# Expert attention in a four-layer decoder: the order of the matmuls in each step, regrouped

## The reference

```python
q = rope(einsum('bsd,hdp->bhsp', x, Wq))
k = rope(einsum('bsd,hdp->bhsp', x, Wk))
gv = gate(x, Wsel_v)                      # sigmoid scores, all but the best 2 of 8 set to 0
v = einsum('bsd,bhse,hedp->bhsp', x, gv, Wv)
att = softmax(einsum('bhsp,bhtp->bhst', q, k) / sqrt(P), axis=-1)
o = einsum('bhst,bhtp->bhsp', att, v)
go = gate(x, Wsel_o)
out = einsum('bhsp,bhse,hepd->bsd', o, go, Wo)
```

## Time and profile before

| | us |
|---|---|
| Median of 3 runs | 2660.39 (2655.98 to 2660.68) |
| The profiled execution | 2660.01 |
| Its span | 2658.2 |
| TensorE busy | 2227.7 (84%) |
| VectorE busy | 1791.3 (67%) |
| ScalarE busy | 1241.8 (47%) |
| GpSimd busy | 1196.4 (45%) |
| Mean granted clock of TensorE | 0.902 of full speed |

### The profile page before, as it was taken

How to read it: one execution, slowest core, us unless ns; L and a number is a source line. 1 busy time by engine, 2 the same in 40 slices (tenths; PEclk the granted TensorE clock), 3 DMA queues, 4 the chain that set the end, 5 groups by cost and what they waited for, 6 DMA issues and landing times. The chain is left out here.

```text
span 2658.2 us, 43969 instructions
## 1 busy us (share of the span) xinstructions
PE 2227.7 (84%) x13502; PEld 1582.2 (60%) x13502; DVE 1791.3 (67%) x3827; ACT 1241.8 (47%) x2557; POOL 1196.4 (45%) x1377
## 2 busy tenths in 40 slices
PE   6888759663999975749999999989999867699698
PEld 3666547453788853636656556655666445499555
DVE  4667658556688856666776676767677555477598
ACT  6777535222566642225445344534444432244365
POOL 5331028001699920127666565756575100022298
PEclk8999869775999998769999999999999977699799
DMA  1000024000666600013344343334333400000184
GB/s 45 2 2 2 7 57 100 7 6 19 140 153 153 150 4 18 1 63 80 80 84 92 77 98 75 96 65 96 77 84 79 87 6 0 32 1 1 25 176 101
DMA packets 63008, 162.17 MB, mean 61 GB/s; under 512 B 7563, under 2 KB 18571, under 8 KB 55000
## 3 DMA queue, kind: packets, MB, share of 16 engines
q1 hardware_dynamic: 62792, 159.50, 26.8%
HBM read 156.46 MB, written 3.01 MB: 60 GB/s over the span
## 5 line engine op out<-in xcount | busy, mean ns | idle before, releaser
L1984 PE MATMUL bank<-l2h_og,l2h_wo 128*128 128x512 f32 x512 | 264.2, 600 | 12.0 <-DVE LNT L2228 11.3
L2086 ACT ACTIVATE l2h_pr<-twin,l2h_nmx 128x512 f32<-128x512 f32 x256 | 176.0, 688 | 173.6 <-PE bank L1973 122.3
L2078 ACT ACTIVATE l2h_prT<-bank 128x512 f32<-128x512 f32 x256 | 151.7, 592 | 213.1 <-PE bank L1973 213.1
L1075 POOL TENSOR_TENSOR l1m_hid_lo<-l1m_hid,l1m_hid_hi 128x512 fp32r<-128x512 f32 x136 | 217.2, 1617 | 62.1 <-ACT l1m_hid_hi L1054 61.4
L2231 DVE TENSOR_REDUCE l2h_nmx<-twin 128x2 f32<-128x1024 f32 x128 | 156.2, 1220 | 104.5 <-PE twin L1963 103.8
L2204 DVE TENSOR_TENSOR l2h_vg<-bank,l2h_gv 128x512 f32<-128x512 f32 x256 | 175.4, 685 | 54.6 <-POOL l2h_vs L2299 32.0
L2299 POOL TENSOR_TENSOR l2h_vs<-l2h_vg 128x256 f32<-128x256 f32 x256 | 190.8, 745 | 27.9 <-DVE l2h_vg L2204 27.7
L2294 POOL TENSOR_TENSOR l2h_plain<-l2h_plain,l2h_rotated 128x512 f32<-128x512 f32 x64 | 82.0, 1281 | 213.9 <-DVE l2h_rotated L2197 213.9
L2216 DVE TENSOR_TENSOR l2h_og<-bank,l2h_gt 128x512 f32<-128x512 f32 x256 | 173.2, 680 | 5.3 <-PE bank L1984 2.7
L1973 PE MATMUL bank<-ident,l2h_pr 128*128 128x128 f32 x1024 | 163.4, 282 | 2.5 <-issue 2.5
L1973 PEld LDWEIGHTS bank<-ident,l2h_pr 128*128 128x128 f32 x1024 | 119.0, 143 | 71.4 <-issue 54.8
(11 more groups left out here) (636 smaller groups left out, 6199.1 us busy)
## 6 DMA issues: line engine op xcount, KB each, us to landing
l2h_gt<-l2m_gate_rows SPq DMA_DIRECT2D x128, 512.0 KB, 7.1
l1m_c<-l1m_weights SPq DMA_DIRECT2D x64, 512.0 KB, 6.3
l3m_c<-l3m_weights SPq DMA_DIRECT2D x32, 512.0 KB, 6.6
l0m_c<-l0m_weights SPq DMA_DIRECT2D x16, 512.0 KB, 6.8
l1m_w<-in_l1m_pairs SPq DMA_DIRECT2D x32, 192.0 KB, 6.2
l2h_fresh<-in_l2m_wqkv SPq DMA_DIRECT2D x8, 768.0 KB, 4.9
l2h_wo<-in_l2m_wo SPq DMA_DIRECT2D x8, 512.0 KB, 4.8
l0m_w<-in_l0m_pairs SPq DMA_DIRECT2D x8, 192.0 KB, 5.0
```

What stands on the lines that cost most here:

```text
L1075: nc.gpsimd.tensor_tensor(hid_lo[:, at, :], hid[:, (n + PRE) % 4, :], hid_hi[:, at, :], ALU.subtract)\
L1984: nc.tensor.matmul(ybank[:, :], wo[s][:, e, :], og[:, e % 4, :], start=(e == 0), stop=(e == E - 1))\
L2078: nc.scalar.activation(prT[:, j // 2 % 2, h, :, j % 2 * P:(j % 2 + 1) * P], tbank[:, :].rearrange("p (c q) -> p c q", c=TPB), ACT.Copy).th ...
L2086: nc.scalar.activation(pr[:, h, :], sbank[:, h, :], ACT.Exp, bias=nmx[:, k % 2, h:h + 1], accum_out=rs[:, g % 2, t, h:h + 1]).then_inc(exp ...
```

## The change

The matmuls of a step are regrouped. The order before was score, turn 0, piece 0, project 0, piece 1, turn 1, piece 2, project 1; it becomes score, piece 0, turn 0, project 0, turn 1, piece 1, piece 2, project 1. What follows (weighing, factor, gates) stays. VectorE's order follows: the second gate product now comes after the third take. No instruction is added or removed, and the waits are those of before, in new places.

```diff
@@ TensorE, step
                         if due(k, 0, last):
                             score(it, k)
+                        for g, n in pieces[0:1]:
+                            make(it, g, n, last)
                         if due(k, 1, last):
                             if 1 <= q <= B and not last:
                                 pe.wait_ge(go_copied, it * B + B + q)
                             turn_probs(it, k - 1, 0)
-                        for g, n in pieces[0:1]:
-                            make(it, g, n, last)
                         if due(k, YLAG, last):
                             project(it, (k - YLAG) // TPB, (k - YLAG) % TPB * 2)
-                        for g, n in pieces[1:2]:
-                            make(it, g, n, last)
                         if due(k, 1, last):
                             turn_probs(it, k - 1, 1)
-                        for g, n in pieces[2:3]:
+                        for g, n in pieces[1:3]:
                             make(it, g, n, last)
                         if due(k, YLAG, last):
                             project(it, (k - YLAG) // TPB, (k - YLAG) % TPB * 2 + 1)
@@ VectorE, step
                         if gates_due:
                             gate(it, (k - OLAG) // TPB, (k - OLAG) % TPB * 2, last)
-                        for g, n in pieces[1:2]:
+                        for g, n in pieces[1:3]:
                             take(it, g, n, last)
                         if gates_due:
                             gate(it, (k - OLAG) // TPB, (k - OLAG) % TPB * 2 + 1, last)
-                        for g, n in pieces[2:3] + factor_at(k, last):
+                        for g, n in factor_at(k, last):
                             take(it, g, n, last)
```

## The result

| | before | after |
|---|---|---|
| Median, us | 2659.22 (4 runs, 2655.98 to 2660.68) | 2682.59 (4 runs, 2678.71 to 2686.38) |
| The profiled execution, us | 2660.01 | 2686.38 (span 2684.6) |
| Ratio after/before | | 1.0089, 95% interval 1.0072 to 1.0107 |

The new order is slower by 23.4 us in the medians, 19 to 28 by the interval. Forecast were 2681 and a range of 2670 to 2692. The profiled execution is the slowest of the four and lies 26.4 us above the profiled one of before, so it shows 3 us more of a difference than the medians do.

The account below looks back on a forecast made before the run. TensorE's own list of work was taken to bound the changed stage: 117 steps x 0.16 = 18.7, +1.8, -3.4, +4.0 make 21.1, less about 0.5: 20.6 us on 2660.39. Forecast 2681, range 2670 to 2692.

Parts of the forecast that it names:

- What bounds the stage: The changed stage: a step lasts as long as TensorE's own list of work; its waits there are small.
- A change of kind costs nothing: TensorE's switches between one-pass (fp32r) and fp32 matmuls: at most 0.01 us each; the 0.15 gap belongs to tile shape.
- Rival (a): Gap behind the scores belongs to the change of kind and goes with it: not slower, 2660 us; chance 0.06.
- Rival (b): Each of four removed changes of kind gives back say 0.08 us: faster, 2643 us; chance 0.03.
- Part 1: Second turn comes too early and waits for ScalarE's copy of the first out of tbank: +0.11 us a step.
- Part 2: A piece instead of the turn follows the scores, exposing a one-pass weight load: +0.05 us a step.
- Part 3: VectorE's gate 1 behind the third take: hidden, except three steps with the weight split, 0.6 us each, +1.8 us.
- rival (c): Gate 1 behind a late third take makes VectorE late in all 42 pick steps: +23 us, 2704; chance 0.05.
- Part 4: Existing TensorE waits for VectorE's LNT add, four step pairs in each of three rounds, swallow lateness: 3.4 us back.
- Part 5: Filling steps 1 to 6, without projection, turns back to back: 5.04 us against 4.26 without weighing, together +4.0 us.
- Rival (d): Longer or shifted TensorE gaps drop the granted clock in one or two more places, 4.7 us each; two or more: 0.08.

Follow-up runs that it names:

- e1: Kernel before the change with only piece 0 moved ahead of turn 0, VectorE's order kept; 2662.25 against 2657.87 us, ratio 1.0021.
- e5: Changed kernel with project 0 moved behind turn 1, so the two turns are adjacent in every step; 2770.22 against 2658.69 us, ratio 1.0421.
- e2: Changed kernel with both projections between the turns, pieces 1 and 2 after them, VectorE's takes in matching order; 2668.07 against 2657.87 us, ratio 1.0042.
- e3: Changed kernel with ScalarE's two waits ahead of the first turn's copy swapped; 2682.83 against 2657.87 us, ratio 1.0097.
- e6: Kernel before the change, but with VectorE in the changed kernel's order; 2664.16 against 2658.69 us, ratio 1.0019.
- e4: Changed kernel with VectorE's order put back to that of before; 2679.78 against 2657.87 us, ratio 1.0092.
- e8: e7 plus VectorE's LNT add moved to the end of the step before, ahead of the pick operation; 2646.27 against 2658.69 us, ratio 0.9958.
- e7: Kernel before the change with the factor's transposes ahead of the weighing, VectorE's factor product waiting for the weighing; 2650.91 against 2658.69 us, ratio 0.9971.

## Why the prediction was right, point by point

**What bounds the stage** held: every edit of TensorE's list showed up in the steady step by its own size (0.05 in e1, 0.84 in e5), edits of VectorE's list did not.

**A change of kind costs nothing**: an even step takes 5.72 with eight alternations, 5.77 with six (e1) and 5.77 with two (e2), and a plain odd step without the factor 7.61, 7.66 and 7.67 with eight, six and four. Rival (a), the gap goes with the kind, is refuted by the load gap of after, 0.66 to the second matmul where (a) wants 0.46. Rival (b) is refuted by e2, which saves as many alternations as the change in odd steps and more in even ones, and gains nothing.

**Part 1 (+0.11)** was right: after minus e1 is 5.88 − 5.77 in an even step. It was mis-sized in odd steps of the loop: after minus e1 is 0.18 there, because the first copy starts later where its two waits stand in that order (e3). The row that I took the price from, in the last four steps, is of written-out code and couldn't show this. Over the 34 plain ones of these steps that is 7.7 − 5.4 = 2.3 of the 4.2 us by which the stage exceeds the forecast.

**Part 2 (+0.05)** was right and measured alone in e1. The Trainium skill (TensorE: Matmul & The Clock Gate, LDWEIGHTS) gives one price to a load of 128 columns; the trace agrees for the one-pass load (2020.35 to 2020.46, 0.11) and not for the transposes (0.06 in the earlier trace rows), and the time followed the rows.

**Part 3** held in kind (nothing in steady steps, rival (c) refuted by e6) and in place (three weight split steps). The size was right too: e4, with the old order, takes 1.85 off the steps 22/23. The 1.38 that e4 leaves there is step 55 at a fallen clock (11.69 against 10.26), which the forecast had not put here. Steps 26/27 cost 1.2 and not 0.5; e4 takes 0.4 off and e6 adds 0.4 by itself, so that much is VectorE's order, and the rest stays open.

**Part 4 (−3.4)** was right where it can be read by itself: steps 14/15 and 18/19 are as long as before (6.10 and 8.09 against 6.10 and 8.06), though TensorE's list in them grew like everywhere.

**Part 5 (+4.0)**: 5.03 for the 5.04 forecast, and +4.48 in all; the two filling steps with weighing lost 0.35 and 1.01 where I took 0.4 each.

**Rival (d)**, the clock, came true in one place of the profiled execution, step 55, at 1.4 us and not 4.7: the clock was at its lower level for a part of the step alone (0.86 in the mean, and 0.59 in the earlier trace rows).

**The total.** The medians differ by 23.4 us where 20.6 were forecast. The base was 1.2 high (2660.4 and then 2659.2 with a fourth run), so the forecast time is 1.6 short and not 2.8. The 20.6 lies inside the interval of 19 to 28 us. The stage of the profiled execution tells more: of its 4.2 us over the forecast, 2.3 are the loop's odd steps, 1.4 the clock in step 55, 0.7 the steps 26/27 and 0.5 the filling, less 0.7 in the other rows of the table. That the base was 1.2 high, and the clock's 1.4 is one execution's, is chance. The profiled executions differ by 26.4: 24.8 from the first to the last scores, and 2.4 less a rest of 0.8 outside, in code that the change doesn't touch (the first scores of the stage come at 1199.56 and 1197.17), which I take for the spread of single executions.

## What to carry to other kernels

Count the changes of tile shape in TensorE's order and the work between two users of one PSUM bank, not the changes between one-pass and fp32 work. A bank that is written, copied out and written again needs the handover's time (here 0.97 us) of other matmuls between the two writes, in every form of the step, the filling ones too. Read that price in the loop's own steps as well as in written-out ones: they differed by 0.07. When the engine that bounds a stage waits a little in a few places, look first for a long operation of a slower engine that one constant can move: here, on top of e8, that took about 9 us from three steps.

## What the runs showed of the hardware that was not expected

- Two waits ahead of one ScalarE instruction: the same code started its copy 0.07 us later in the loop than written out (0.27 against 0.20 behind the projection), and swapping the two waits turned that round (e3). What carries the 0.07 isn't shown.
- Adjacent fp32r and fp32 matmuls of one tile shape cost each other at most 0.01 us; a change of shape costs 0.15 to 0.22. Into 128 x 128 work the gap goes with how far apart the first two weight loads come: 0.15 with 0.06 (transposes), 0.20 with 0.11 (one-pass loads).
- The granted clock after gaps of TensorE of 1.9 to 3.0 us fell to its lower level in some rounds and held in others, with the same work, at 1.0 to 1.6 us each (11.88 against 10.26 in before, 11.37 against 10.40 in e8). The longest gaps (3.0, in e7) had a fall in one round of three.
